# Windowed attention in float32 on one core: the weights are loaded behind five rows of x, and the rings hold a row's two halves side by side

## The reference

```python
xn = (x - mean_g) / sqrt(var_g + eps)            # 32 groups of 8 channels, over a whole image
q, k, v = split(einsum(xn, qkv_w) + qkv_b)       # 256 channels each
regions = 7 x 7 windows of 8 x 8 pixels
idx = top_k(mean(q) @ mean(k), 4)                # for each region, the 4 nearest by region means
out = softmax(q * 256**-0.5 @ k[idx].T) @ v[idx] # 8 heads of 32, 64 queries and 256 keys a region
out = out + depthwise3x3(v) + lepe_b
return x + einsum(out, out_w) + out_b
```

## Time and profile before

| | |
|---|---|
| three runs | 1755.33, 1755.62, 1763.09 us |
| median | 1755.62 us |
| profiled execution, its own time | 1761.20 us |
| its span, first to last instruction | 1759.1 us |
| PE busy | 1643.8 us, 93% |
| DVE, ACT, POOL busy | 87%, 78%, 61% |
| DMA | 234.43 MB, mean 133 GB/s |
| q1 (SP) | 141408 packets, 129.71 MB |
| q0 (POOL) | 22864 packets, 100.02 MB |

### The profile page before, as it was taken

One profiled execution on the slowest core, in us unless ns is written; L12 is line 12 of the kernel. 1 busy time (PEld: TensorE's weight loads), 2 busy tenths in 40 slices (PEclk: granted clock), 3 DMA queues, 4 the chain that ended last, 5 costly groups with the idle time before them and its releaser, 6 DMA issues.

```text
span 1759.1 us, 73643 instructions
## 1 busy us (share of the span) xinstructions
PE 1643.8 (93%) x26568; PEld 1374.0 (78%) x26568; DVE 1532.4 (87%) x2951; ACT 1380.3 (78%) x4401; POOL 1064.4 (61%) x2548
## 2 busy tenths in 40 slices
PE   4999999999999999899999999999999999999897
PEld 4878887888778887788778887788787888777676
DVE  6589898999889999889898989899898888889895
ACT  2488887888888888788778888888887888877674
POOL 3256565666566665666566666666656666667654
PEclk9999999999999999999999999999999999999999
DMA  6233434353434343434344444434433333456555
GB/s 203 79 98 118 135 112 136 110 153 124 125 114 140 113 154 115 131 111 132 118 130 125 128 135 119 130 119 137 127 121 109 112 111 115 147 172 221 184 178 191
DMA packets 164632, 234.43 MB, mean 133 GB/s; under 512 B 19232, under 2 KB 146912, under 8 KB 164272
## 3 DMA queue, kind: packets, MB, share of 16 engines
q1 hardware_dynamic: 141408, 129.71, 25.1%
q0 software_dynamic: 22864, 100.02, 16.9%
HBM read 166.80 MB, written 62.85 MB: 131 GB/s over the span
## 4 chain that ended last, share of the span: by engine, by line
PE 71%; DVE 11%; ACT 6%; issue 6%; DMA 2%; SPq 2%; POOL 1%; POOLq 0%; DVEq 0%; ACTq 0%
PE chunk_bank L1144 22%; PE pt_bank L1260 13%; PE s_bank L1238 11%; PE o_bank L1278 8%; PE chunk_bank L1158 5%; DVE neg_max L976 5%; ACT probs L759 4%; PE o_bank L1260 4%; DVE lepe L863 3%; PE o_bank L1286 3%; PE chunk_bank L1186 2%; PE chunk_bank L1171 2%; DMA v_sel<-v_dram 1%; SPq L458 1%; ACT probs_t L769 1%
## 5 line engine op out<-in xcount | busy, mean ns | idle before, releaser
L759 ACT ACTIVATE probs<-s_bank,neg_max 128x256 f32<-128x256 f32 x1568 | 733.3, 482 | 232.4 <-DVE neg_max L976 232.4
L517 POOL COPY k_sel<-k_all 128x128 f32 x1568 | 403.4, 305 | 469.3 <-PE s_bank L1238 385.2
L863 DVE SCALAR_TENSOR_TENSOR lepe<-v_band,taps,lepe 128x448 f32<-128x448 f32 x896 | 621.6, 744 | 0.0
L976 DVE TENSOR_REDUCE neg_max<-s_bank 128x2 f32<-128x512 f32 x784 | 486.9, 683 | 130.0 <-PE s_bank L1238 129.0
L1144 PE MATMUL chunk_bank<-xn,wqkv 128*128 128x224 f32 x2544 | 577.6, 356 | 7.7 <-issue 4.9
L1144 PEld LDWEIGHTS chunk_bank<-xn,wqkv 128*128 128x128 f32 x2544 | 442.6, 191 | 9.5 <-issue 4.6
L769 ACT COPY probs_t<-pt_bank 128x512 f32<-128x512 f32 x611 | 366.0, 599 | 52.3 <-PE pt_bank L1260 51.3
L1260 PE MATMUL pt_bank<-ident,probs 128*128 128x128 f32 x2444 | 380.1, 278 | 28.5 <-ACT probs L759 16.0
L1260 PEld LDWEIGHTS pt_bank<-ident,probs 128*128 128x128 f32 x2444 | 276.6, 141 | 123.1 <-issue 71.6
L529 POOL TENSOR_TENSOR lepe<-o_norm,lepe 128x128 f32<-128x128 f32 x392 | 268.3, 704 | 147.9 <-DVE o_norm L999 144.5
L759 ACT ACTIVATION_READ_ACCUMULATOR probs<-s_bank,neg_max 128x1 f32 x1568 | 331.7, 212 | 0.0
(11 more groups left out here) (81 smaller groups left out, 1451.5 us busy)
## 6 DMA issues: line engine op xcount, KB each, us to landing
v_sel<-v_dram SPq DMA_DIRECT2D x1568, 64.0 KB
xn<-x_dram POOLq DMA_DIRECT2D x56, 448.0 KB, 4.6
v_dram<-v_stage SPq DMA_DIRECT2D x112, 224.0 KB
resid<-x_dram POOLq DMA_DIRECT2D x31, 448.0 KB, 4.3
out_dram<-resid POOLq DMA_DIRECT2D x31, 448.0 KB, 3.8
spill<-lepe POOLq DMA_DIRECT2D x25, 448.0 KB, 3.6
xn<-spill POOLq DMA_DIRECT2D x25, 448.0 KB, 6.0
resid<-x_dram POOLq DMA_DIRECT2D x25, 224.0 KB, 3.2
```

The source lines that it names most:

```text
L517: last = pool.tensor_copy(k_sel[:, r % K_SLOTS, :, RT * j:RT * (j + 1)], k_all[:, b % 2, :, bass.ds(reg[j] * RT, RT)])
L759: act.activation(probs[:, 2 * (j % 2) + i, :], s_bank[:, u, KEYS * at:KEYS * (at + 1)], ACT.Exp, bias=neg_max[:, h % 2, col:col + 1], accu ...
L863: ins = dve.scalar_tensor_tensor(row, v_band[:, n % BANDS, k, t // 3:t // 3 + RS, t % 3:t % 3 + W], taps[:, k, t:t + 1], row, ALU.mult, AL ...
L976: dve.tensor_reduce(neg_max[:, h % 2, 2 * j:2 * j + 2], scored, AX.X, ALU.max, negate=True).then_inc(max_done, 1)
```

## The change

The dimensions of the two rings are swapped, from [partition, half, slot, pixel] to [partition, slot, half, pixel], in all their uses; a row's two halves of 1792 bytes then form one run of 3584 bytes in a partition. SP issues group first, with a semaphore of its own, then waits until row 4 of x has landed, and issues wqkv, bqkv, ident, btap, taps, wout and bout on `weights_in`. PE waits for group alone before the group means, and for `weights_in` before the first projection; its wait for ident at the very start is gone. DVE makes the image's constants first and waits for the weights behind them, in `prepare`. The count N_WEIGHTS stays at 7.

```diff
-        xn = sb("xn", [P, KC, X_RING, ROW])
+        xn = sb("xn", [P, X_RING, KC, ROW])
...
-        lepe = sb("lepe", [P, KC, LEPE_RING, ROW])
+        lepe = sb("lepe", [P, LEPE_RING, KC, ROW])
...
-            sp.dma_start(ident[:], ident_d).then_inc(ident_in, 16)
-            sp.dma_start(group[:], group_d).then_inc(weights_in, 16)
+            sp.dma_start(group[:], group_d).then_inc(group_in, 16)
+            sp.wait_ge(x_loaded[4], 16)
+            sp.dma_start(wqkv[:], w_qkv.rearrange("(k p) o -> p k o", p=P)).then_inc(weights_in, 16)
             sp.dma_start(bqkv[:], b_qkv).then_inc(weights_in, 16)
+            sp.dma_start(ident[:], ident_d).then_inc(weights_in, 16)
+            sp.dma_start(btap[:], b_tap).then_inc(weights_in, 16)
             sp.dma_start(taps[:], w_tap).then_inc(weights_in, 16)
-            sp.dma_start(btap[:], b_tap).then_inc(weights_in, 16)
-            sp.dma_start(wqkv[:], w_qkv.rearrange("(k p) o -> p k o", p=P)).then_inc(weights_in, 16)
             sp.dma_start(wout[:], w_out.rearrange("(k p) o -> p k o", p=P)).then_inc(weights_in, 16)
             sp.dma_start(bout[:], b_out).then_inc(weights_in, 16)
...
-                cells = lepe[:, :, g % LEPE_RING, :].rearrange("p k (r c) -> p k r c", c=W)[:, :, :, cols]
+                cells = lepe[:, g % LEPE_RING, :, :].rearrange("p k (r c) -> p k r c", c=W)[:, :, :, cols]
...
-                pool.dma_start(xn[:, :, n % X_RING, :], x[n]).then_inc(x_loaded[n % X_RING], 16)
+                pool.dma_start(xn[:, n % X_RING, :, :], x[n]).then_inc(x_loaded[n % X_RING], 16)
...
-                pool.dma_start(spill[LATE.index(g)], lepe[:, :, g % LEPE_RING, :]).then_inc(spilled, 16)
+                pool.dma_start(spill[LATE.index(g)], lepe[:, g % LEPE_RING, :, :]).then_inc(spilled, 16)
...
-                pool.dma_start(xn[:, :, slot, :], spill[LATE.index(g)]).then_inc(late_in[slot], 16)
+                pool.dma_start(xn[:, slot, :, :], spill[LATE.index(g)]).then_inc(late_in[slot], 16)
...
+            image_constants(0)
             prepare()
-            image_constants(0)
...
-            pe.wait_ge(ident_in, 16)
-
...
                 if b == 0:
-                    pe.wait_ge(weights_in, 16 * N_WEIGHTS)
+                    pe.wait_ge(group_in, 16)
...
             group_means(0)
             group_vars(0)
+            pe.wait_ge(weights_in, 16 * N_WEIGHTS)
```

More of the change, by code:

```diff
@@ L318, in attention_kernel @@
                       pt_bank[:, :]]
-        ident_in, weights_in, idx_in = map(sem, ("ident_in", "weights_in", "idx_in"))
+        group_in, weights_in, idx_in = map(sem, ("group_in", "weights_in", "idx_in"))
         x_loaded = [sem(f"x_loaded{i}") for i in range(X_RING)]
@@ L539, in mid_tap @@
                         wait_full(pool, "out", n - LEPE_RING, 1)
-                pool.tensor_scalar(in_image(lepe[:, k, n % LEPE_RING, :]),
+                pool.tensor_scalar(in_image(lepe[:, n % LEPE_RING, k, :]),
                                    v_band[:, n % BANDS, k, 1:1 + RS, 1:1 + W], taps[:, k, MID_TAP:MID_TAP + 1],
@@ L576, in normalize @@
                 pool.wait_ge(x_read, x_reads(n))
-                row = xn[:, k, n % X_RING, :]
+                row = xn[:, n % X_RING, k, :]
                 pool.tensor_scalar(row, row, rstd[:, k:k + 1], shift[:, k:k + 1], ALU.mult, ALU.add
@@ L861, in outer_tap @@
                     dve.wait_ge(lepe_step, tap_at[n, k])
-                row = in_image(lepe[:, k, n % LEPE_RING, :])
+                row = in_image(lepe[:, n % LEPE_RING, k, :])
                 ins = dve.scalar_tensor_tensor(
@@ L879, in x_moments @@
                 wait_x(dve, n)
-                dve.bn_stats(stats[:, k, rr, :], xn[:, k, n % X_RING, :]).then_inc(x_read, 1)
+                dve.bn_stats(stats[:, k, rr, :], xn[:, n % X_RING, k, :]).then_inc(x_read, 1)
             def x_sums(n, k):
@@ L889, in x_sums @@
                 dve.tensor_reduce(x_sum[:, k, rr * NWIN:(rr + 1) * NWIN],
-                                  xn[:, k, n % X_RING, :].rearrange("p (r g c) -> p g r c", r=RS, g=NWIN), AX.XY,
+                                  xn[:, n % X_RING, k, :].rearrange("p (r g c) -> p g r c", r=RS, g=NWIN), AX.XY,
                                   ALU.add).then_inc(x_read, 1)
@@ L904, in normal_sums @@
                 ins = dve.tensor_reduce(xn_sum[:, k, n * NWIN:(n + 1) * NWIN],
-                                        xn[:, k, n, :].rearrange("p (r g c) -> p g r c", r=RS, g=NWIN), AX.XY, ALU.add)
+                                        xn[:, n, k, :].rearrange("p (r g c) -> p g r c", r=RS, g=NWIN), AX.XY, ALU.add)
                 if n == LAST and k == KC - 1:
@@ L1144, in project @@
                     ins = pe.matmul(bank_of(kind, n, k)[:, cols], wqkv[:, part, col:col + P],
-                                    xn[:, part, n % X_RING, cols], start=(part == 0), stop=(part == KC - 1))
+                                    xn[:, n % X_RING, part, cols], start=(part == 0), stop=(part == KC - 1))
                 if last == QUARTERS:
@@ L1158, in project_out @@
                     ins = pe.matmul(bank_of("out", g, m)[:, cols], wout[:, part, P * m:P * (m + 1)],
-                                    lepe[:, part, g % LEPE_RING, cols], start=(part == 0), stop=(part == KC - 1))
+                                    lepe[:, g % LEPE_RING, part, cols], start=(part == 0), stop=(part == KC - 1))
                 if last == QUARTERS:
@@ L1170, in project_late @@
                         wait_bank(pe, "late", g, 1)
-                    ins = pe.matmul(bank_of("late", g, 1)[:, cols], wout[:, part, P:2 * P], xn[:, part, slot, cols],
+                    ins = pe.matmul(bank_of("late", g, 1)[:, cols], wout[:, part, P:2 * P], xn[:, slot, part, cols],
                                     start=(part == 0), stop=(part == KC - 1))
```

## The result

The changed kernel took 1764.98 us in the median of 8 runs (1759.93 to 1767.37), the kernel before 1755.79 us in 8 runs of the same sitting. The ratio is 1.0049, with a 95% interval of 1.0031 to 1.0067: slower by 8.6 us, between 5.4 and 11.8. The prediction was 1758 in a range of 1751 to 1764, so both the time and the size of the change were outside it. The profiled execution took 1764.61 us for a span of 1762.6, near the median.

A forecast was written before the change was run, and what follows sets the result against it. PE was taken to bound the kernel, busy 93% of the span and 71% of the chain of waits. The start's +2.5 us and 0 behind it, put on the median of 1755.62, gave 1758 us, range 1751 to 1764.

The forecast's parts named there:

- Steps 1 and 2: Start: x rows load without weights beside them, moments done at 13.7 to 14.2 us, scale ready 4.4 us earlier at most.
- Step 3: Start: weights alternate one for one with x rows 7 to 13, land at 24.8 us; first normalisation 2.5 us later.
- Rival A: Start: SyncE's queue gets more than one packet per x packet, weights land in time; 1753 us, chance 0.2.
- Step 4: Middle of the kernel: larger pieces shorten x landings and POOL's issues, but nobody waits for them; 0 us.
- 0 behind it: Everything after the start: steady part, tail and engine instructions on new strides together change the time by 0.
- Step 5: Tail: late rows slow the v_sel gathers by 1.7 us at most, POOL's shorter issues offset it; 0, within 2 us.
- rival B: Tail: gather packets alternate with larger late-row packets, v_sel landings over 10 us each; 1767.7 us, chance 0.1.
- Rival C: Tail: POOL's shorter issues and add free the gathers of keys, some 3 us below forecast; 1755 us, chance 0.1.
- The forecast of the start: Start: first normalisation 2.5 us later, waiting for the weights, and passed on one for one to the end.
- The sign of the change: Whole kernel: slower by 2.5 us, though within the 8.8 us a measurement can tell; same 0.90, slower 0.06, faster 0.04.

The follow-up runs named there:

- rings_only: Only the two rings' dimensions swapped, order of issue at the start as before, against the kernel before: ratio 1.0039, in a second sitting 1.0054.

## Why the prediction was wrong

**Steps 1 and 2, the early rows.** Right, somewhat too fast: row 0 at 5.18 us (5.3 predicted), row 4 at about 10.97 (10.1; SyncE's issue at 10.99 shows it), moments done at 14.4 (13.7 to 14.2), scale at 18.6 (18.1).

**Step 3, the weights.** The landing of 24.46 us against 24.8, and the first normalisation 2.1 us later against 2.5, were right. The way there was not: the counts of 12 to 22 us are 549 to 669, not far from even, but they came as 437 to 239 and then 112 to 430. The landing held because it hangs on the total of bytes, the bound that the step gave. What it missed is that the same queueing already depends on the rings: `rings_only` shows the weights 2.8 us later at DVE's wait with the old order. With rows 7 to 13 behind the weights the landing comes at 16.8 us, below the 17.5 that the step gave, without a working, for weights served first.

**Rival A** (weights in time) did not come: until 20 us SyncE's queue got fewer packets than x's, not more. The Trainium skill, in DMA: Bandwidth & Descriptors, section Queues, rings and completion order, has the engines go round the queues packet by packet, and its rule put the weights last; the landing agrees, the even turns show in neither of the two stretches.

**Step 4, the rings in the steady part,** is the step that failed, together with the sum's "0 behind it". The packets (19,472 in q0 against 22,864) and POOL's shorter issues came as predicted. But "no engine waits for an x load, so the landing is worth nothing" was taken to mean that the rings cost nothing. The runs show 3.2 ± 1.1 us in their place, of which 1.7 us stand in POOL's closing drain, 8.58 us instead of 6.87; the other 1.5 ± 1.1 are not placed. The prediction had named two places where a change of loads can move the time, the start and a transfer on the chain. It put nothing at a third, the end behind the last store, and did not list the 6.87 us that POOL drains there in the trace before, although they go into the time in full.

**Step 5, the tail.** v_sel holds 11.5% of the chain from 1500 us on against 9.0%, in four pieces of 6.8 to 8.0 us instead of three. PE waits 5.7 us for it instead of 4.6. The landings are not longer, as forecast; rival B, with over 10 us each, did not happen. Over the seven traces with both rings new and the nine with both old, these waits of PE behind 1535 us average 5.1 and 4.0 us; at that spread it is a hint of 1 us, no more. **Rival C** did not happen either.

The forecast of the start was the whole of the sum, and it covers a third of what was measured: 2.3 of 6.9 us. That each us of the start is passed on was right (0.94 ± 0.18). The sign of the change was right and its size was not. The first sitting gave more than all sittings together, 8.6 us by its ratio against 6.9. With 6.9 us the time would have been near 1763, inside the range; that it fell outside is in part chance, that the sum lacked over 4 us is not. The range also had little room for the spread of single executions (standard deviation 3.6 us), of which falls of the clock are a large part.

**What stays open.** Of the 6.9 us, 2.3 are the start and 1.7 the closing drain. The other 2.9 are not placed: the fit gives 1.5 ± 1.1 us to the rings and 1.7 ± 1.0 to the order of issue behind its start. The profiled executions do not show the rings' part: from the first maximum to 1535 us they last 1450.5 us with new rings and 1450.9 with old, with 1.3 and 1.6 falls. It is also open why POOL's drain is longer with both rings and not with one. That PE's stalls marked issue are waits for instructions was not shown by an experiment: only that loads of queue q8, marked instruction, run beside them, 214 of 16 KB in the span, one every 8 us or so.

A version that beats both kernels: the new order of issue, x rows 7 to 13 behind the weights, old rings. Its 24 runs give 1754.0 us in the median, 1.8 ± 1.4 us under the kernel before by the means and 8.7 under the changed one. With the lepe ring alone changed, 12 runs gave 0.9976 (0.9958 to 0.9994).

## What to carry to other kernels

Moving a transfer behind others helps whoever waits for the others, and hurts by the total of bytes that now stand before it: look for what else sits in the other queue, here seven rows that nobody needed for 20 us, and hold those back first. Read what stands behind the last useful instruction as well as what stands before the first one: here 1.7 us of the loss were in a drain that no busy row lists, the same in every trace, while the times needed dozens of runs to show it. Where a change is worth a few thousandths, read the granted clock in several executions of the kernel before, and leave out the part behind the last matmul, where a low clock lowers the mean and costs nothing. A control that only delays the start told more than repeating the parts.

## What the runs showed of the hardware

- PE's granted clock fell to 1.2 GHz at the end of a stall of 2.16 us in the middle of dense work and was back after 3.4 us, at an estimated price of 1.7 us. The stall's length did not decide: 1.90 us brought a fall in one execution and none in another, and 3.0 us brought none in a third.
- POOL's drain at the end of the program took 8.58 us where both rings were changed and 6.87 us in every other kernel here. The last store had landed 4 us before it ended.
- Loads of the same bytes to the same partitions cost another queue differently by the size of their pieces: with x in 80 instead of 112 packets a row, the last of eight weight transfers took 16.8 us to land instead of 14.1.
- POOL issued a load with pieces of 3584 bytes in 550 ns and one with pieces of 1792 in 728 ns.
